# Turning six of sixteen blocks by SBUF transfers and VectorE transposes instead of on TensorE

## The reference

```python
def _L0_cond_ref(hidden_states, language_ids, W1, b1, W2, b2, gamma, beta):
    w1 = W1[language_ids]
    w2 = W2[language_ids]
    h = jnp.einsum('bsh,bha->bsa', hidden_states, w1) + b1[language_ids][:, None, :]
    h = jax.nn.relu(h)
    adapted = jnp.einsum('bsa,bah->bsh', h, w2) + b2[language_ids][:, None, :]
    x = hidden_states + adapted
    mean = jnp.mean(x, axis=-1, keepdims=True)
    var = jnp.mean(jnp.square(x - mean), axis=-1, keepdims=True)
    normed = (x - mean) * jax.lax.rsqrt(var + LN_EPS)
    return normed * gamma[language_ids][:, None, :] + beta[language_ids][:, None, :]

def _L1_cond_ref(x, cat_ids, W, b):
    out = jnp.einsum('bsd,bdh->bsh', x, W[cat_ids]) + b[cat_ids][:, None, :]
    return out

x = x + _L0_cond_ref(x, itok_B_0_8, ...)    # x: (8, 1024, 512) float32, W1: 512x128, W2: 128x512
x = x + _L1_cond_ref(x, itok_B_0_63, ...)   # W: 512x512
```

## Time and profile before

| | |
|---|---|
| median of 3 runs | 314.22 us (314.17 to 314.31) |
| span of the profiled execution, first to last instruction | 312.3 us |
| median less that span | 1.9 us |
| PE busy | 303.9 us, 97% of the span |
| PEld, DVE, ACT, POOL busy | 244.4, 225.6, 211.1, 225.8 us |
| DMA | 65.39 MB, mean 209 GB/s |
| share of PE in the chain of work that ended last | 92% |

### The profile page before, as it was taken

How to read it: one execution, slowest core, us unless ns; L and a number is a source line. 1 busy time by engine, 2 the same in 40 slices (tenths; PEclk the granted TensorE clock), 3 DMA queues, 4 the chain that set the end, 5 groups by cost and what they waited for, 6 DMA issues and landing times.

```text
span 312.3 us, 4810 instructions
## 1 busy us (share of the span) xinstructions
PE 303.9 (97%) x1424; PEld 244.4 (78%) x1424; DVE 225.6 (72%) x641; ACT 211.1 (68%) x381; POOL 225.8 (72%) x185
## 2 busy tenths in 40 slices
PE   8988999999999999999999999999999999999995
PEld 8424678888888888888888888888888888888884
DVE  0185989696986869598686969778695977889610
ACT  1045667886696958778596857958686874857431
POOL 0649685999779995999959996899959995541000
PEclk9999999999999999999999999999999999999999
DMA  6999795778766798768867888677867381111122
GB/s 199 338 364 370 237 338 176 218 233 284 216 172 212 207 297 250 182 185 258 275 192 197 232 256 247 154 215 246 303 202 198 111 300 37 67 67 71 67 101 101
DMA packets 40943, 65.39 MB, mean 209 GB/s; under 512 B 6100, under 2 KB 10196, under 8 KB 40916
## 3 DMA queue, kind: packets, MB, share of 16 engines
q1 hardware_dynamic: 40336, 64.03, 66.2%
q10 hardware_dynamic: 580, 1.05, 1.1%
HBM read 48.29 MB, written 16.78 MB: 208 GB/s over the span
## 4 chain that ended last, share of the span: by engine, by line
PE 92%; DVE 4%; ACT 2%; issue 1%; POOL 0%; POOLq 0%
PE out_ps L778 54%; PE down_ps L778 14%; PE h_ps L778 13%; PE turn_ps L833 9%; PE turn_ps L904 2%; DVE y L488 1%; ACT y L376 1%; DVE stats L493 1%; DVE turn_ps L532 0%; DVE x1T_lo L539 0%; ACT w_hi L347 0%; ACT hT L358 0%; ACT out_sb L394 0%; DVE mean_var L497 0%; ACT w_hi L341 0%
## 5 line engine op out<-in xcount | busy, mean ns | idle before, releaser
L778 PE MATMUL out_ps<-x1T_hi,w_hi 128*128 128x512 f32 x256 | 100.4, 392 | 0.0
L778 PE MATMUL out_ps<-x1T_lo,w_hi 128*128 128x512 f32 x256 | 99.8, 390 | 0.0
L778 PE MATMUL out_ps<-x1T_hi,w_lo 128*128 128x512 f32 x256 | 99.7, 389 | 0.0
L687 POOL TENSOR_TENSOR xrow<-xrow,b_rows 128x512 f32<-128x512 f32 x64 | 82.6, 1294 | 9.3 <-DMA xrow<-x_rows 9.3
L385 ACT ACTIVATE x1T_hi<-turn_ps,gamma_beta 128x512 fp32r<-128x512 f32 x64 | 43.2, 689 | 43.7 <-DVE turn_ps L532 43.7
L532 DVE SCALAR_TENSOR_TENSOR turn_ps<-turn_ps,gamma_beta,xT 128x512 f32<-128x512 f32 x64 | 45.4, 754 | 34.4 <-PE turn_ps L833 33.5
L376 ACT ACTIVATE y<-y,shift,rstd 128x512 f32<-128x512 f32 x64 | 52.2, 818 | 20.4 <-DVE shift L523 20.0
L692 POOL TENSOR_TENSOR xT_lo<-xT,xT_hi 128x512 fp32r<-128x512 f32 x48 | 62.4, 1300 | 4.7 <-ACT xT_hi L328 4.7
L488 DVE TENSOR_TENSOR y<-down_ps,xrow 128x512 f32<-128x512 f32 x64 | 43.7, 683 | 19.6 <-PE down_ps L778 19.5
L778 PEld LDWEIGHTS out_ps<-x1T_hi,w_hi 128*128 128x128 f32 x256 | 48.1, 188 | 10.9 <-issue 0.8
L778 PEld LDWEIGHTS out_ps<-x1T_hi,w_lo 128*128 128x128 f32 x256 | 48.1, 188 | 10.1 <-issue 0.2
(11 more groups left out here) (40 smaller groups left out, 356.8 us busy)
## 6 DMA issues: line engine op xcount, KB each, us to landing
xrow<-x_rows SPq DMA_DIRECT2D x32, 512.0 KB, 6.7
out_cols<-out_sb SPq DMA_DIRECT2D x64, 256.0 KB, 2.6
xT<-x_cols SPq DMA_DIRECT2D x30, 512.0 KB, 6.2
w<-w_all SPq DMA_DIRECT2D x8, 1024.0 KB, 7.2
w<-w_all SPq DMA_DIRECT2D x15, 256.0 KB, 5.2
b_rows<-b_all SPq DMA_DIRECT2D x8, 256.0 KB, 8.1
xT<-x_cols ACTq DMA_DIRECT2D x4, 256.0 KB, 4.6
w<-w_all SPq DMA_DIRECT2D x4, 64.0 KB, 3.7
```

What stands on the lines that cost most here:

```text
L687: nc.gpsimd.tensor_tensor(xrow[:, i % XR, :], xrow[:, i % XR, :], b2_rows[:, m % 2, :], ALU.add).then_inc(rowbias_done, 1)
L778: mm = nc.tensor.matmul(out, lhsT, rhs, start=first and n == 0, stop=last and n == len(terms) - 1)
```

## The change

Six blocks, 3, 5, 7, 9, 11 and 13 (`SHUFFLED`), are no longer turned by TensorE. When all four tiles of such a block are normalised, SP issues 16 DMAs inside SBUF (`shuffle`), each of 32 rows by four tiles by 128 columns (64 KB in rows of 512 bytes), which move 32-row quadrants of `y` into a new buffer `z`. VectorE then transposes 32x32 squares of `z` into `turn_ps` (`flip`, one per tile), and goes on with `merge` and `x1_low` as before. The first two flips of a block stand at the end of VectorE's step 4b+6, with their `merge` and `x1_low` (a `late` step), the other two at the head of step 4b+7. From tile 12 on, `out`, `finish` and `store` come one step later, for all blocks; step 19 holds no `out`. `y` of these blocks is written in another order of columns by `add_rows`, so that the squares come out right. ScalarE normalises a shuffled block's last tile at the head of step 4b+4. The output has three buffers in place of four, and in a late step SP issues `load_cols` last.

```diff
-    OUT = -7
-    FINISH = -8
-    LAST = TILES - 1 - FINISH
+    SHUFFLED = range(3, BLOCKS - 1, 2)
+    Q = P // BLOCK
+    LATER = SHUFFLED[0] * BLOCK
+    def out_at(s):
+        i = s - 7 if s - 7 < LATER else s - 8
+        return i if 0 <= i < TILES and (s - 7 < LATER or s - 8 >= LATER) else None
+    def finish_at(s):
+        return out_at(s - 1)
...
-        return (first, first + 1) if there(first) else ()
+        return (first, first + 1) if there(first) and first // BLOCK not in SHUFFLED else ()
+    def flipped(s):
+        first = {2: s - 6, 3: s - 5}.get(s % BLOCK, -1)
+        return (first, first + 1) if there(first) and first // BLOCK in SHUFFLED else ()
...
-        XC, XR, WR, OS = 16, 8, 8, 4
+        XC, XR, WR, OS = 16, 8, 8, 3
+        z = sb("z", [P, BLOCK, BLOCK, P])
...
+            def shuffle(blk):
+                sp.wait_ge(norm_done, BLOCK * (blk + 1))
+                if shuffled_before(blk):
+                    sp.wait_ge(flip_done, BLOCK * shuffled_before(blk))
+                r = blk * BLOCK % WR
+                for g in range(BLOCK):
+                    for q in range(BLOCK):
+                        sp.dma_start(z[q * Q:(q + 1) * Q, :, g, :],
+                                     y[g * Q:(g + 1) * Q, r:r + BLOCK, q * P:(q + 1) * P]).then_inc(shuffled, 16)
...
-                if there(s + FINISH):
-                    store(s + FINISH)
+                if s % BLOCK == 0 and s // BLOCK - 1 in SHUFFLED:
+                    shuffle(s // BLOCK - 1)
+                if finish_at(s) is not None:
+                    store(finish_at(s))
+                if cols and late:
+                    load_cols(s + LOAD_COLS)
...
+            def flip(i):
+                k = i % KC
+                dve.wait_ge(shuffled, 16 * BLOCK * BLOCK * (shuffled_before(i // BLOCK) + 1))
+                dve.wait_ge(x1lo_done, i - 1)
+                nc.vector.transpose(turn_ps[i % 2][:], z[:, :, :, k * Q:(k + 1) * Q]).then_inc(flip_done, 1)
...
-                tiles = turned(s)
+                late = s % BLOCK == 2 and len(flipped(s)) > 0
+                tiles = () if late else (*turned(s), *flipped(s))
                 if tiles:
+                    for i in flipped(s):
+                        flip(i)
                     for i in tiles:
                         merge(i)
...
+                if late:
+                    for i in flipped(s):
+                        flip(i)
+                    for i in flipped(s):
+                        merge(i)
+                    for i in flipped(s):
+                        x1_low(i)
```

More of the change, by code:

```diff
@@ L63, in turned, with shuffled_before, turns, flips @@
         first = {1: s - 5, 2: s - 4}.get(s % BLOCK, -1)
-        return (first, first + 1) if there(first) else ()
+        return (first, first + 1) if there(first) and first // BLOCK not in SHUFFLED else ()
+    def flipped(s):
+        first = {2: s - 6, 3: s - 5}.get(s % BLOCK, -1)
+        return (first, first + 1) if there(first) and first // BLOCK in SHUFFLED else ()
+    def shuffled_before(blk):
+        return len([b for b in SHUFFLED if b < blk])
+    def turns(i):
+        return i + 1 - BLOCK * shuffled_before(i // BLOCK)
+    def flips(i):
+        return BLOCK * shuffled_before(i // BLOCK) + i % BLOCK + 1
     with ExitStack() as ctx:
@@ L283, in step @@
             def step(s):
-                if s % 2 == 0 and XC <= s + LOAD_COLS < TILES:
+                cols = s % 2 == 0 and XC <= s + LOAD_COLS < TILES
+                late = s % BLOCK == 2 and len(flipped(s)) > 0
+                if cols and not late:
                     load_cols(s + LOAD_COLS)
@@ L450, in step @@
             def step(s):
+                first = s % BLOCK == 0 and s // BLOCK - 1 in SHUFFLED
+                late = s % BLOCK == 2 and len(flipped(s)) > 0
+                if first:
+                    normalise(s + NORM)
                 for i in turned(s):
                     x1_high(i)
-                if there(s + FINISH):
-                    finish(s + FINISH)
+                if not late:
+                    for i in flipped(s):
+                        x1_high(i)
+                if finish_at(s) is not None:
+                    finish(finish_at(s))
                 if (s + UP) % BLOCK == BLOCK - 1 and there(s + UP):
@@ L460, in step @@
                     h_high((s + UP) // BLOCK)
-                if there(s + NORM):
+                if there(s + NORM) and not first:
                     normalise(s + NORM)
@@ L484, in add_rows @@
                 dve.wait_ge(rowbias_done, i + 1)
[L485 to L489, removed]
+                before = i // BLOCK - WR // BLOCK
+                if before in SHUFFLED:
+                    dve.wait_ge(shuffled, 16 * BLOCK * BLOCK * (shuffled_before(before) + 1))
+                elif before >= 0:
+                    dve.wait_ge(turn_done, turns(before * BLOCK + BLOCK - 1))
+                out, in0, in1 = y[:, i % WR, :], down_ps[i % 2][:], xrow[:, i % XR, :]
+                if i // BLOCK in SHUFFLED:
+                    out = out.rearrange("p (q k c) -> p k q c", q=BLOCK, k=KC)
+                    in0, in1 = (a.rearrange("p (k q c) -> p k q c", q=BLOCK, k=KC) for a in (in0, in1))
+                nc.vector.tensor_tensor(out, in0, in1, ALU.add).then_inc(y_done, 1)
             def statistics(i):
@@ L898, in step @@
                     up(s + UP)
-                if there(s + OUT):
-                    out(s + OUT)
+                if out_at(s) is not None:
+                    out(out_at(s))
             pe.wait_ge(ident_done, 1)
@@ L905, in _ @@
             opening()
-            for s in range(OPEN, TILES - OUT):
+            for s in range(OPEN, LAST):
                 step(s)
```

11 lines of the change are left out of this document (9 added, 2 removed).

## The result

| | before | after |
|---|---|---|
| median | 314.20 us (4 runs) | 354.96 us (4 runs, 351.97 to 356.65) |
| ratio | | 1.130, 95% interval 1.125 to 1.136 |
| span of the profiled execution | 312.3 us | 353.2 us |
| mean granted clock of TensorE | 1.00 | 0.94 |

The changed kernel is slower, as forecast, but by 40.8 us where 13.6 were forecast; the time lies above the range. The page of the changed kernel's profile has these lines; they answer to the earlier trace rows.

What follows compares the result with a forecast made beforehand. TensorE, busy 97% of the span, was taken as the bound: 312.3 - 10.7 (transposes) + 6 x 3.59 (waits) + 2.72 (empty step 19) = 325.9 us, with 1.9 us for median over span 327.8; range 316 to 345.

Steps and rivals of the forecast that it cites:

- What it takes away: TensorE: two steps per shuffled block lose their eight transposes, 1.79 us per block, 10.7 us over six blocks.
- VectorE's run: Block 7, from the plain part of step 34 through flips, merges and `x1_low`: `x1_low(31)` ends at +20.44 from step 32's start.
- late flips at +11.32: VectorE, block 7: flips start when step 34's plain part ends, 11.32 us after the start of step 32.
- the rival of two passes: VectorE's flips take two passes each, a pair 2.56 us; 344.0 us in all, chance 0.10.
- The estimate by the Trainium skill's figure: Skill's VectorE transpose figure, 311 ns, scaled to four times the columns: flip 1.24 us, pair about 2.5, sum some 343 us.
- The wait at `out`, and the chain behind it: TensorE per shuffled block: 2.76 us at `out` for `x1_low(31)`, then 0.83 at the next `turn`, 3.59 together.
- An issue takes 0.36 us, sixteen 5.8; ... +10.5, hidden: SP's shuffle transfers: last issued from +6.8, landed 3.7 us later at +10.5, before the flips at +11.32; costed at nothing.
- My price for it: Shuffle landing later than +11.32 from step 32's start: each microsecond past it costs 6 us in all.
- this case: Rival that the shuffle lands late and flips wait on the transfers: landing at +13.3 gives 340 us; chance 0.12.
- a cover of 0.8 us: Margin between the shuffle's forecast landing at +10.5 and the end of step 34's plain part at +11.32.
- `out` one step later: TensorE's work conserved, except that step 19 holds no `out`, so block 3's wait is 2.72 us longer, once.
- Stores and loads behind the shuffle: SP's later stores (needed 12 us later) and `load_cols` (over two steps' lead) cost nothing; otherwise ScalarE would wait.

Runs made afterwards that it cites:

- run 10: Changed kernel without the transfers, `finish` ahead of the late `x1_high` and eleven filler matmuls before the late `out`; 329.27 us, ratio 1.050 to the kernel before.
- run 5: Changed kernel, nothing left out, with ScalarE's `finish` ahead of the flipped `x1_high` and 22 filler matmuls before the wait at `out`; 347.48 us, ratio 1.109.
- run 1: Changed kernel without the 16 transfers per block, flips reading `y`'s own quadrants; 333.12 us, ratio 1.062 to the kernel before.
- run 7: Changed kernel with `SHUFFLED` empty, all blocks turned by TensorE, `out` still one step later from tile 12 on; 315.60 us, ratio 1.0062.
- run 2: Changed kernel with all 16 issues, each moving two of four tiles from the second shuffled block on; 351.70 us, ratio 1.123.
- run 4: Changed kernel with thirteen filler matmuls into `out_ps` ahead of the wait for `x1_low`, the output-buffer wait moved ahead of them; 361.60 us, ratio 1.153.

## Why the prediction was right in sign and wrong in size

The runs share the miss out: 327.8 us forecast, 329.3 without transfers and without the fall of the clock (run 10), 347.5 with the transfers (run 5), 355.0 with the fall too. So 1.5, 18.2 and 7.5 us; by the excess over the kernel before, run beside each (13.6 forecast, 15.8, 34.0, 40.8), 2.2, 18.2 and 6.8. The split depends on the order: taking the transfers out first (run 1) gives 21.8 us for them and 3.9 for the clock.

- **What it takes away.** Right as far as is seen: steps without turns took 4.08 us as before, and run 10's total fits 10.7 us for all.
- **VectorE's run.** Right to 0.1 us: late flips at +11.32 forecast, +11.24 in run 10 (161.70); from there to the end of `x1_low(31)` 9.12 forecast, 9.08 there and 9.09 in the changed kernel. A pair of flips spans 1.32 us, back to back with the next operation about 1.2 as taken; a single one is 703 ns, and with that the rival of two passes falls. The estimate by the Trainium skill's figure ("VectorE: DVE Perf Modes", section "The three transpose paths"), 1.24 us a flip, is not borne out.
- **The wait at `out`, and the chain behind it.** Right without late transfers: 2.69 to 2.70 us (run 1) for 2.76, and 3.57 us a block by `turn` (run 10: +23.97 less +20.40) for 3.59.
- **The step that failed: "An issue takes 0.36 us, sixteen 5.8; ... +10.5, hidden".** I took the issue of a load from DRAM; an issue of the shuffle takes 0.60 us. (The row of 0.36 us is `load_w2`, 256 KB, and not one of the 64 KB loads whose 3.7 us stand beside it; those took 0.33 to 0.40 us, so the slip changed little.) The last issue began at +11.54 in place of +6.8, and though it landed in 2.02 us and not in 3.7, that was +13.56 in block 7, and the flips began at +13.59. My price for it (each microsecond past +11.32 costs 6 us in all) was right: 2.27 us there lengthened the wait by 2.30, and the flips' waits in six blocks (16.0 us, 16.5 in run 5) are most of the 18.2. I had priced this case at 340 us and given it 0.12; a cover of 0.8 us under sixteen unmeasured issues did not deserve more trust than that.
- **The term that was missing: the clock.** The prediction priced waits by their length alone and put the slower matmuls behind them at nothing. Behind 5.06 us of standing, twelve matmuls took 5.07 us instead of 2.72. Less the turn wait that they cover, this cost about 7 us in all (run 5), and 3.9 in the version without transfers (run 1 to run 10).
- **`out` one step later.** 2.72 forecast, 2.1 alone (run 7); in block 3 of run 10, 0.91 at `up` and 1.54 more than block 7 at `out`, 2.45 in all. The sum had no term for the 1.37 us at block 13.
- **Stores and loads behind the shuffle.** Costed at nothing; right in so far as no wait of TensorE in the changed kernel was released by `finish`.

## What to carry to other kernels

A short cover (here 0.8 us) under work that the trace has no row for is a coin toss: price the case that it fails, and if that is many times the gain, let it weigh in the forecast. DMA issues on one queue were serial work of the issuing engine here (sixteen took 10.8 us), so count them like instructions and take their duration from the same kind of transfer, not from the same number of bytes. A wait of TensorE costs more than its length where the clock falls behind it, and in run 1 equal waits did not always bring that fall. And where a consumer is moved later to hide a late producer, look at what else stands behind the producer in each in-order list: here the wait went from `out` to `finish`, to a weight copy, to `up`, and only the move of the weight copy gave back a good part of the loss.

## What the runs showed of the hardware that was not expected

- SP took 0.36 us to issue a 256 KB load from DRAM, 0.33 to 0.40 us for a 64 KB one in 512-byte rows (the four at the start of the kernel before), and 0.60 us for a 64 KB move within SBUF in 512-byte pieces, on 32 partitions; half the bytes left it at 0.60 (run 2). What in these shapes makes the difference was not tried.
- With the issues on two queues the landing took 5.4 us in the median, with one 2.9, for the same transfers.
- The length of a wait did not by itself tell whether the clock fell. After 2.70 us without a matmul `out` ran slow in part in two blocks (4.39 and 4.50 us for 2.72) and at full clock in two others (run 1); after 3.67 us the filler of run 4 ran at full clock in block 7; after 5.06 us `out` ran slow nearly throughout (5.07). What else decides was not tried.
- The Trainium skill warns of idle gaps between bursts of matmuls, behind which TensorE is back at its lower clock ("TensorE: Matmul & The Clock Gate", section "Why this matters for your kernels"); the changed kernel's trace agrees, with a granted clock of 0.56 behind the wait of 5.06 us, and so does run 5, with 1.00 throughout where filler ran in it.
